# Layer 2 cross-attention on one core: the order of TensorE's work at the border of two batches

## The reference

```python
K = jnp.einsum('bse,hed->bhsd', context, Wk2)      # 32 x 16 x 1500 x 8
V = jnp.einsum('bse,hed->bhsd', context, Wv2)
Q = jnp.einsum('bqe,hed->bhqd', a, Wq2)            # 32 x 16 x 56 x 8
scores = jnp.einsum('bhqd,bhkd->bhqk', Q, K)
att = jax.nn.softmax(scores / jnp.sqrt(sk), axis=-1)
out = jnp.einsum('bhqk,bhkd->bhqd', att, V)
return jax.nn.relu(out.transpose(0, 2, 1, 3).reshape(...) @ Wo2 + bo2)
```

## Time and profile before

| | |
|---|---|
| three runs, median | 4118.23 us |
| lowest and highest | 4118.02 and 4121.68 us |
| span of the profiled execution, first to last instruction | 4105.3 us |
| median of the runs less that span | 12.9 us |
| TensorE busy in the span | 3514.6 us (86%) |
| VectorE, ScalarE, GpSimd busy | 2402.2, 1828.7, 1040.3 us |
| mean granted TensorE clock | 0.907 of full |
| stage L2b: first and last score product | 2629.4 and 3321.3 us |

### The profile page before, as it was taken

How to read it: one execution, slowest core, us unless ns; L and a number is a source line. 1 busy time by engine, 2 the same in 40 slices (tenths; PEclk the granted TensorE clock), 3 DMA queues, 4 the chain that set the end, 5 groups by cost and what they waited for, 6 DMA issues and landing times. The chain is left out here.

```text
span 4105.3 us, 78007 instructions
## 1 busy us (share of the span) xinstructions
PE 3514.6 (86%) x30578; PEld 2463.3 (60%) x30578; DVE 2402.2 (59%) x4475; ACT 1828.7 (45%) x3354; POOL 1040.3 (25%) x583
## 2 busy tenths in 40 slices
PE   6977995999999999999987998699999973358859
PEld 4654443788787787878864777355555532235534
DVE  2434332676676676767753443688888845546545
ACT  1422221555555555555542544266565621125516
POOL 0000001111111111111101120377777730025406
PEclk6998996999999999999998998799999985569969
DMA  3621001011001001001001665333333300045300
GB/s 71 128 55 62 0 0 52 31 40 38 32 32 44 34 32 47 32 32 39 31 14 46 242 233 207 78 90 84 92 93 85 89 2 6 0 75 106 61 12 23
DMA packets 155620, 253.45 MB, mean 62 GB/s; under 512 B 11159, under 2 KB 114852, under 8 KB 155012
## 3 DMA queue, kind: packets, MB, share of 16 engines
q1 hardware_dynamic: 155268, 248.49, 21.6%
HBM read 173.81 MB, written 74.65 MB: 61 GB/s over the span
## 5 line engine op out<-in xcount | busy, mean ns | idle before, releaser
L1813 DVE TENSOR_SCALAR_CACHE_REDUCE L_p<-L_score,L_cols 128x1500 f32<-128x1500 f32 x224 | 398.7, 1780 | 383.4 <-PE L_score L1649 383.4
L1752 ACT CAST L_pthi<-L_pt 125x512 bf16<-125x512 f32 x672 | 350.2, 594 | 541.0 <-PE L_pt L1658 541.0
L2095 ACT ACTIVATE L2b_p<-L2b_score 125x448 f32<-125x448 f32 x768 | 391.6, 542 | 290.2 <-PE L2b_score L2010 282.7
L1669 PE MATMUL L_acc<-L_chi,L_pthi 125*128 125x128 bf16 x2688 | 462.2, 220 | 0.4 <-DVE L_attn L1833 0.4
L1671 PE MATMUL L_acc<-L_chi,L_ptlo 125*128 125x128 bf16 x2688 | 461.7, 219 | 0.0
L1670 PE MATMUL L_acc<-L_clo,L_pthi 125*128 125x128 bf16 x2688 | 461.6, 219 | 0.0
L1826 DVE TENSOR_TENSOR L_ptlo<-L_pt,L_pthi 125x512 bf16<-125x512 f32 x672 | 418.2, 678 | 1.1 <-ACT L_pthi L1752 1.1
L1736 ACT ACTIVATE L_p<-L_p,L_least 128x1500 f32<-128x1500 f32 x224 | 350.4, 1564 | 7.1 <-DVE L_p L1813 5.2
L1658 PEld LDWEIGHTS L_pt<-ident,L_p 128*125 128x125 f32 x2688 | 327.8, 188 | 32.5 <-ACT L_p L1736 1.1
L1658 PE MATMUL L_pt<-ident,L_p 128*125 128x128 f32 x2688 | 330.0, 273 | 0.5 <-ACT L_p L1736 0.4
L2166 DVE TENSOR_REDUCE L2b_max<-L2b_m 112x1 f32<-112x1000 f32 x256 | 301.8, 1192 | 35.1 <-PE L2b_m L1991 34.9
(11 more groups left out here) (554 smaller groups left out, 7046.6 us busy)
## 6 DMA issues: line engine op xcount, KB each, us to landing
L2b_kst<-L_keys SPq DMA_DIRECT2D x96, 375.0 KB, 5.6
L_ctx<-dram_ctx SPq DMA_DIRECT2D x32, 750.0 KB
L_ct<-L_ct SPq DMA_DIRECT2D x32, 750.0 KB
L2a_ct<-L_ct SPq DMA_DIRECT2D x32, 750.0 KB, 14.1
L_keys<-L2a_kout SPq DMA_DIRECT2D x32, 750.0 KB, 7.5
L_values<-L2a_vout SPq DMA_DIRECT2D x32, 750.0 KB
L2b_vin<-L_values SPq DMA_DIRECT2D x32, 750.0 KB
L0x_ctx<-dram_ctx SPq DMA_DIRECT2D x32, 672.0 KB
```

Source lines behind the costliest of these rows:

```text
L1669: pe.matmul(acc, pt_hi[k % 2][:, t, :], c_hi[half][:, t, :], start=(t == 0), stop=False)
L1752: act.copy(pt_hi[k % 2][:, 4 * j:4 * j + 4, :], pt_ps[j][0:KP, :].rearrange("p (t q) -> p t q", t=4)).then_inc(hi_done, 1)
L1813: dve.tensor_scalar(probs[k % 2][:, :].rearrange("p (i n) -> p i n", i=3), score_ps[:, :].rearrange("p (i n) -> p i n", i=3)[:, :, 0:500], ...
L2095: act.activation(probs[t % RP][:, half * 2 * GW:(half + 1) * 2 * GW], score_ps[half][0:KP, 0:2 * GW], ACT.Exp).then_inc(exp_done, 1)
```

## The change

TensorE's list no longer treats the end of a batch apart. The scores run one tile ahead of the slots through the border too, and `weighted` with its `sums` follows one tile behind, through a new `behind(g)` that counts tiles over all batches:

- S0 and S1 move from behind G2 to between N1 and W10 (slot 33 and 34 are empty).
- S2, M0 and S3 move from behind G3 to ahead of W11, O11 and G3.
- ScalarE's `exps` of the first five tiles of a batch wait for GpSimd's addition that reads the buffer last (tiles 6 to 10 of the batch before), because the order no longer ensures it.
- `EARLY` is 0 and leaves the plan and the prologue as they were; the order on VectorE, GpSimd and the DMA queue stays.

```diff
--- before.py
+++ after.py
@@ -1881,14 +1881,16 @@
 
 
     MAXSLOT = (0, 2, 5, 7, 10, 12, 15, 17, 20, 22, 25, 27)
-    PLAN = [(MAXSLOT[n], "max", n, f"m{n % 2}", 1) for n in range(MAXU)]
+    EARLY = 0
+    PLAN = [(MAXSLOT[n], "max", n, f"m{n % 2}", 2 if n < EARLY else 1) for n in range(MAXU)]
     PLAN += [(6, "query", 0, "u", 2), (13, "out", 0, "u", -1), (18, "negmax", 0, "u", 1), (32, "negmax", 1, "u", 1)]
     PLAN.sort(key=lambda x: x[0])
     PROLOGUE = [("query", 0, "u", 0), ("query", 0, "u", 1)]
-    for n in range(MAXU):
-        PROLOGUE.append(("max", n, f"m{n % 2}", 0))
-        if n % 6 == 5:
+    for n in range(MAXU + EARLY):
+        PROLOGUE.append(("max", n % MAXU, f"m{n % 2}", n // MAXU))
+        if n % 6 == 5 and n < MAXU:
             PROLOGUE.append(("negmax", n // 6, "u", 0))
+    LATE = 1
     BUFS = ("u", "m0", "m1")
 
     def sum_steps(j):
@@ -2049,24 +2051,26 @@
                 pe.wait_ge(w_loaded, 16 * 3)
                 for kind, k, f, n in PROLOGUE:
                     unit(kind, k, n)
+                def behind(g):
+                    b, t = divmod(g, KT)
+                    weighted(b, t)
+                    if t in (4, 7, 10):
+                        sums(b, (4, 7, 10).index(t))
+
                 scores(0, 0)
                 scores(0, 1)
                 for b in range(B):
                     for t in range(KT):
-                        if t + 1 < KT:
-                            scores(b, 2 * t + 2)
+                        g = KT * b + t
+                        scores((g + 1) // KT, 2 * ((t + 1) % KT))
                         slot(b, 3 * t)
-                        if t + 1 < KT:
-                            scores(b, 2 * t + 3)
+                        scores((g + 1) // KT, 2 * ((t + 1) % KT) + 1)
                         slot(b, 3 * t + 1)
-                        if t > 0:
-                            weighted(b, t - 1)
-                        if t in (5, 8, 11):
-                            sums(b, (5, 8, 11).index(t))
+                        if g >= LATE:
+                            behind(g - LATE)
                         slot(b, 3 * t + 2)
-                    scores(b + 1, 0)
-                    scores(b + 1, 1)
-                    weighted(b, KT - 1)
+                for g in range(KT * B - LATE, KT * B):
+                    behind(g)
                 unit("out", 0, B - 1)
 
             @block.scalar
@@ -2091,6 +2095,8 @@
                         wait(act, av_done, KT * b + t - RP + 1)
                         if t >= RP:
                             act.wait_ge(sum_step, STEPS * b + added(t - RP))
+                        elif b > 0 and t + RP < KT - 1:
+                            act.wait_ge(sum_step, STEPS * (b - 1) + added(t + RP))
                     act.wait_ge(scores_full, HALVES * b + s + 1)
                     act.activation(probs[t % RP][:, half * 2 * GW:(half + 1) * 2 * GW], score_ps[half][0:KP, 0:2 * GW],
                                    ACT.Exp).then_inc(exp_done, 1)
```

## The result

The changed kernel takes 4192.66 us (median of 4 runs, 4186.86 to 4196.95), the kernel before 4118.12 us beside it (4 runs, 4109.6 to 4121.68): a ratio of 1.0188, 95% interval 1.0172 to 1.0205. It is slower by about 75 us where 46 were forecast, and lies above the range. The profiled span went from 4105.3 to 4185.1 us.

The account below looks back on a forecast made before the run. Bound: TensorE's ordered work from N1 to G3, VectorE's chain from G3 to M3 (5.56 us), then TensorE again. G3 1.49 us later at 31 borders adds 46.2 us to 4118.2, giving 4164.4; range 4146 to 4182.

Parts of the forecast that it names:

- the first term: TensorE, N1 to G3: G3 starts 1.49 us later at each of 31 borders, 46.2 us in all.
- the second and the third: G3 to M3 stays 5.56 us, VectorE's chain; TensorE's granted clock stays 1.00: both add nothing.
- The sum's second part: Ahead of G3 on TensorE: S2, M0 and S3 now come first and delay G3 by 0.95 us.
- E0: ScalarE's exponential that S2 waits for at the border; started 0.51 us after S0, forecast to add nothing.
- G3 to M3 still 5.56: VectorE's chain from G3 to M3 at the border keeps its length, 0.63 + 4.93 = 5.56 us.
- the same phase to each other: From M3 on, all waits keep their relative timing, so nothing is added there.
- The forecast's bound above: S1's wait for N1 at twice its size, 1.08 us: 31 x 2.03 = 63 us, 4181.
- The slack: Rival: TensorE's 1.47 us wait behind G3 absorbs moved work; 4134.9 (chance 0.05), or no change, 4118 (chance 0.03).
- "Faster": Rival: earlier S0 to S3 remove the border waits at M2 and M3; 45.6 us less, 4072.7; chance 0.03.
- The clock rival: More TensorE idling at the border lowers its clock: 1.5 us lost at each of 31 borders, 47 us, 4211; chance 0.05.

Follow-up runs that it names:

- The first move: Only S0 and S1 moved ahead of W10; against the changed kernel, W11, O11 and G3 return ahead of S2: 4131.18 us, ratio 1.0055.
- the second move: Only S2, M0 and S3 moved ahead of W11; against the changed kernel, S0 and S1 return behind G2: 4190.74 us, ratio 1.0193.

## Why the prediction was wrong

The direction, the place and the mechanism of the first term held. The size of the whole did not; the sum's terms one by one, of which the second and the third failed:

- *N1 to G3, forecast 1.49 us later, measured 1.56.* Its parts hold: S1 waits for N1, S2, M0 and S3 lie ahead of G3. The first move was sized at 0.54 and costs 0.47 alone. The sum's second part, 0.95, holds only together with the first: alone the second move costs 1.55 us there (N1 at 2963.60, G3 at 2967.58), because S2 waits for E0.
- *"G3 to M3 still 5.56" failed:* 5.87. The step was "the same phase to each other". I took L2b_heads at the 0.77 us of the row without asking what it waits for; the instruction is worth 0.22. In the kernel before it ended 0.07 us behind the first of GpSimd's two additions there (3288.11 to 3290.19). With the new order the exponentials of S0 to S3 come earlier relative to OH, the first addition is over in time, and heads runs into the second one, which starts at once when E5 is there. Over 29 borders 9 us.
- *The clock was given a chance of 0.05,* on the ground that one border of the kernel before held 1.00 with 4.02 busy us of 5.50. That row was of the thirtieth border alone, which has no `query` unit; the usual one is busier (4.73 of 5.50 below), and the change takes work out of just this piece (3.76 of 5.86 above). So the sum had the clock at nothing. As a price of the rival I had 1.5 us at every border; measured were 4.6 to 6 us at four of 31, 21 us in all.

```profile
2980.20:2985.70 5.50, 4.73 (x46) 2.89 (x38) 4.72 (x9) 3.33 (x7) 3.18 (x2) 1.00 0.72 147
```

With these terms the sum is 56 + 21 = 77 us, of the span's 79.8; the medians differ by 75. The forecast's bound above, 63 us, had doubled the wrong term: the wait for N1, which was right.

The rivals. The slack took none of the moved work: it could not, M3 hanging on OH. "Faster" fell for the reason given. Its price of 45.6 us took the thirtieth border's waits (0.16 and 1.31 us) for those of all; the usual ones are 0.16 and 0.66, 25.1 us in all, and taking those at M3 away won 26 us. The clock rival was half true: right in what would happen, in the wrong number of places.

The rule of the Trainium skill on short idle times between groups of matmuls (TensorE: Matmul & The Clock Gate, "A second HAM failure mode: psum-queue depth-cycling"), which I had weighed against one row, is borne out: at two of the four drops no wait of the border was longer than 0.97 us. That matmuls keep their order is borne out by S1: W10 starts 1.19 us behind S0 in the changed kernel (2970.22 to 2971.41), and with S1 moved behind it 0.30 us (3003.45 to 3003.75).

## What to carry to other kernels

When work is moved ahead of a product, look for the engine that waits for that product, not for the one that does the work. Before pricing a chain on another engine by a row's duration, compare the end of each of its rows with the ends on the engine beside it: a duration may be a wait in disguise, and then it changes with the phase. Taking work out of a stretch in which TensorE waits can cost more than the stretch, by its clock; compare the windows of the stretch before and after.

## What the runs showed of the hardware

- VectorE's product of two tensors in on-chip memory (128x56) took 0.22 us between GpSimd's instructions, and 0.77, 1.08, 1.51 and 2.06 us in kernels in which GpSimd's addition was running, ending 0.06 to 0.09 us behind it at every border read. The Trainium skill (SBUF — State Buffer, "Who interferes with whom") says that a VectorE instruction with two SBUF inputs contends with a GpSimd instruction that reads SBUF, and that the port pair which they share is an exclusive lock; the trace agrees. The reductions from PSUM, 1.19 us, didn't lengthen beside GpSimd.
- TensorE's clock fell at the end of a wait of 0.97 us that followed waits of 0.67 and 0.47 in the same stretch, and stayed at 1.2 GHz for ten us, though TensorE was busy without a gap. A drop cost 4.6 us as a rule. Of the changed kernel's borders the two with the longest waits at M3 (1.25 and 1.62 us) had a drop, and two of those with 0.97; with M0's reduction first the wait at M3 was 1.51 us at nearly every border, and six had a drop. So the length of one wait doesn't decide it. Why a drop comes at some borders and not at others that look alike stays open, and so does what the even distance of seven borders in one kernel comes from.
- Repeating matmuls whose result is there already, inside a wait, kept the clock at 2.4 GHz and made the kernel 18 us faster than without them (ratios 1.0144 and 1.0188).
